# Projecting two head pairs at once in an attention and feed-forward kernel

## The chip, the cores and the metric

The kernel runs on one core of a Trainium2 chip. The metric is the device time of one execution in microseconds (us); lower is better. A core has five engines that run side by side and meet at semaphores: TensorE (PE; its weight loads are listed apart, as PEld), VectorE (DVE), ScalarE (ACT), GpSimd (POOL) and SyncE (SP), which here only starts DMA transfers. Sums of products land in PSUM, which has eight banks of 512 float32 values in each of 128 partitions.

## The reference, cut to what matters

Four batches of 1024 rows with 128 columns are normalised; the result goes through causal attention with 16 heads of width 64 and, beside it, through a quantised layer with ternary weights. Everything is float32.

```python
x = L0_attn_query                       # (4, 1024, 128)
xn = _layernorm(x)
# attention, B=4, S=1024, H=16, DH=64
q, k, v = split_heads(xn @ Wq), split_heads(xn @ Wk), split_heads(xn @ Wv)
w = softmax(einsum('bhqd,bhkd->bhqk', q, k) / DH + causal)
w = w * clip((arange(s) + span_val * s) / (RAMP + 1), 0, 1)
w = w / (sum(w, -1) + 1e-8)
attn = merge_heads(einsum('bhqk,bhkd->bhqd', w, v)) @ Wo      # Wo (1024, 128)
# feed-forward
x_int = clip(round(xn / scale), -127, 127)
ffn = nan_to_num(x_int * scale) @ (ternary_weight - 1).T + bias
return x + attn + ffn
```

The product with `Wo` is a sum over heads. A pair of heads gives 128 of its 1024 inputs, and the kernel adds what each pair brings to the rows of `x`.

## The kernel before, in words

The work is cut into 32 head pairs (8 for each batch), and one round of the program handles a pair. Each engine has a written order of units for a round (`PE_PLAN`, `ACT_PLAN`, `DVE_PLAN`, `POOL_PLAN`, lines 36 to 41), other orders for the start (`PE_FIRST` and so on) and for the last round (`PE_LAST`, `POOL_LAST`). A plus behind a unit means the next pair, a minus the pair before; `walk` writes the orders out.

The units, with their lines: Q and K project the queries and keys (881 to 885); M0 to M11 are the products from which the row maxima come (912), which DVE's R0 to R11 read (732, 736); V makes the values (899 to 901) and DVE's Vs weighs them (718); S0 to S11 are the scores of one block of keys (939), which ACT's E0 to E11 turn into `prob` (541); POOL's L cuts the diagonal blocks (448) and its A sums `prob` for the denominators (471, 475); G3, G7 and G11 are the products of `prob` with the values (956); D0 and D1 the denominators of the two halves of the queries (968); DVE's o divides (768) into `o_sb`; Y0 and Y1 are the output projection of a half (995), and DVE's Ya0 and Ya1 add it to `x_sb` (777). In the last pair of a batch the feed-forward products (983) go into the same bank ahead of Y.

Six PSUM banks form `ring`, three slots of two banks. The units Q, K, M, V and S take the slots in the order of the program, so each waits until the unit three places before it has been read (`slot_left`): behind S by its exponential, behind M by its maxima. In the middle of a round that order is S5 S6 M5 M6 M7 S7 M8, later S8 S9 S10 M9 M10 M11 S11. The bank `beside` carries T, D, X, W, F and Y one after the other (`beside_left`); `pv` takes the products of `prob` with the values. Y reads `o_sb`, one buffer for each half.

Units of a round on PE, around the change: `S5 S6 M5+ Y1- M6+ M7+ S7 D0 G3 M8+ S8 S9 S10 M9+ Y0 M10+ M11+ S11 G7`. A Y is four float32 products, each of which runs as two instructions.

At the start PE computes the maxima of pair 0 with idle products between them, I0 to I8 (1001): products of constants whose result is not used, two instructions each. `xn_sb` holds all four normalised batches, and parts of it first hold the raw weights `w_raw` and `wv_raw`, from which POOL makes the low parts `w2` (398) and `wv2` (431).

Of the kernel before, what the change touches and what calls it, by code (L numbers as in the profile page):

```python
# [32 lines left out]

PE_PLAN = ("T Q+ K+ X0 X1 W G11- M0+ M1+ S0 S1 S2 M2+ D1- M3+ V+ S3 S4 M4+ S5 S6 M5+ Y1- M6+ M7+ S7 D0 G3 "
           "M8+ S8 S9 S10 M9+ Y0 M10+ M11+ S11 G7")
ACT_PLAN = "Z Qhi+ Khi+ X0 X1 E0 E1 E2 ln1- ex1- E3 E4 E5 E6 E7 ln0 ex0 E8 E9 E10 E11"
# [1 line left out]
            "R9+ R10+ Ya0 R11+ Rc+")  # L40
POOL_PLAN = "L0 A0 L1 A1 L2 A2 L3 A3 A4 A5 A6 A7 L8 L9 L10 L11 A8 A9 A10 A11 B"

PE_FIRST = ("Q+ K+ M0+ M1+ M2+ I0+ M3+ I1+ M4+ I2+ M5+ I3+ M6+ I4+ M7+ I5+ M8+ I6+ M9+ I7+ M10+ I8+ M11+ Q++ T+ "
            "K++ S0+ S1+ S2+ V+")
DVE_FIRST = ("Qlo+ Klo+ R0+ R1+ R2+ R3+ R4+ R5+ R6+ R7+ R8+ R9+ R10+ R11+ Rc+ Tc+ Qlo++ Klo++ keys+ Vs+")
ACT_FIRST = "xf0+ Qhi+ xf1+ Khi+ rest+ keys+ wv+ Qhi++ Khi++ E0+ E1+ E2+"
# [13 lines left out]


STEP_OF = {1: "stats1", 2: "var1+", 3: "norm1a", 4: "norm1b", 5: "stats2", 6: "stats3", 7: "var2",
           8: "rstd2", 9: "norm2a", 10: "norm2b", 11: "norm3a", 12: "norm3b"}


def happens(name, i):

    if name in ("X0", "X1"):
        return i % PAIRS_OF_BATCH == 4 + int(name[1:]) and i < N_PAIRS - PAIRS_OF_BATCH
    if name == "W":  # L70
        return i == 1
    if name == "F1":
        return i == LAST
    if name[0] == "I":
        return i == 0
    if name == "q":
        return i % PAIRS_OF_BATCH < PAIRS_OF_BATCH - 1
    if name == "Z":
        return i in STEP_OF
    if name == "B":  # L80
        return i in (6, 11, 14)
    if name == "store":
        return i % PAIRS_OF_BATCH == PAIRS_OF_BATCH - 1
    return True
# [43 lines left out]
def attention_ffn(nc, x_dram, wq_dram, wk_dram, wv_dram, wo_dram, span_dram, tern_dram, bias_dram,  # L128
# [11 lines left out]
    with ctx:  # L140
# [4 lines left out]
            return ctx.enter_context(nc.semaphore(name))  # L145

        x_sb = sb("x_sb", [P, NB, D])
        xn_sb = sb("xn_sb", [P, NB * P])
        x1 = [sb(f"x1_{n}", [P, S], F32R) for n in range(2)]
        x2 = [sb(f"x2_{n}", [P, S], F32R) for n in range(2)]  # L150
        xf = sb("xf", [P, S])
        fq = sb("fq", [P, S])

        w_raw = [xn_sb[:, (B - 2 + n) * S:(B - 1 + n) * S] for n in range(2)]
        wv_raw = xn_sb[:, S:2 * S]
# [17 lines left out]
        v_sb = [sb(f"v_{p}", [P, KB, 4, DH]) for p in range(2)]  # L173
        NPROB = 8
        prob = [sb(f"prob_{n}", [P, 2, HALF]) for n in range(NPROB)]
        psumd = [sb(f"psumd_{c}", [P, 2, HALF]) for c in range(2)]

        minus_one, plus_one = psumd[0][0:1, :, :], psumd[1][0:3, :, :]
        lnden = sb("lnden", [P, HALF])
        r0 = sb("r0", [P, HALF])  # L180
        rden = sb("rden", [P, HALF])
        o_sb = [sb(f"o_{c}", [P, HALF]) for c in range(2)]
        rowmax = [sb(f"rowmax{p}", [P, P]) for p in range(2)]
        rowmax2 = [sb(f"rowmax2_{p}", [P, 2, HB]) for p in range(2)]
        maxrow = sb("maxrow", [2 * KB, P], F32R)
# [119 lines left out]
        def _(sp):  # L305
# [52 lines left out]
            for name, i in walk(SP_PLAN, SP_FIRST):  # L358
                if name == "mrow":
                    place_maxrow(i, i % 2)  # L360
                elif name == "kext":
                    place_key_weights(i, i % 2)
                else:
                    b = i // NPB
                    sp.wait_ge(y_added, halves_upto(i, 0))
                    store(b, 0, HB)
                    sp.wait_ge(y_added, halves_upto(i, 1))
                    store(b, HB, KB)
            sp.wait_ge(out_stored, 16 * 2 * B)

# [1 line left out]
        def _(pool):  # L372
# [105 lines left out]
            for name, i in walk(POOL_PLAN, "", POOL_LAST):  # L478
                if name[0] == "L":
                    select(i, int(name[1:]))  # L480
                elif name[0] == "A":
                    add(i, int(name[1:]))
                else:
                    add_bias((6, 11, 14).index(i) + 1)

        @block.scalar
        def _(act):
# [109 lines left out]
        def _(dve):  # L597
# [29 lines left out]

            def normalise(b, n0, n1):
                for n in range(b * KB + n0, b * KB + n1):
                    v.tensor_scalar(xn_sb[:, n * P:(n + 1) * P], x_sb[:, n, :], mv[:, n, 0:1],  # L630
                                    rstd[:, n:n + 1], ALU.subtract, ALU.mult).then_inc(xn_done, 1)

            def turned(b, c, src):
# [19 lines left out]

            def quantise(b, step):

                over = xn_sb[:, b * S:(b + 1) * S].bitcast(U32)
                if b or step > 1:
                    dve.wait_ge(fq_step, b * FQ_STEPS + (step - 1))
                else:
                    dve.wait_ge(lnw_split, 2)  # L660
                if step == 1:
                    dve.wait_ge(xf_done, 2 * b + 2)
                    ins = v.tensor_scalar(fq[:, :], xf[:, :], sc[:, 5:6], ACT_QB, ALU.mult, ALU.min)
                elif step == 2:
# [12 lines left out]

            def layer_norm_rest(step):

                if step[:5] == "stats":  # L680
                    statistics(int(step[5:]))
                elif step == "var1+":
                    variances(KB, 2 * KB)
                    rstd_finish(2, slice(KB, 2 * KB))
                elif step == "var2":
                    variances(2 * KB, NB)
                elif step == "rstd2":
                    rstd_finish(3, slice(2 * KB, NB))
                else:
                    if step == "norm1a":  # L690
                        dve.wait_ge(w_lo_done, 4)
                        dve.wait_ge(wv_lo_done, 1)
                    n0 = HB * "ab".index(step[5])
                    normalise(int(step[4]), n0, n0 + HB)

            def key_weights():

# [66 lines left out]
            def normalise_values(i, c):  # L764

                dve.wait_ge(rden_done, halves_upto(i, c))
                dve.wait_ge(pv_done, tiles_upto(i, HB - 1 if c == 0 else NT - 1))
                v.scalar_tensor_tensor(out=o_sb[c][:, :], in0=pv[:, :], scalar=-1.0, in1=rden[:, :],  # L768
                                       op0=ALU.mult, op1=ALU.mult).then_inc(o_done, 1)

            def add_output(i, c):

                b = i // NPB
                dve.wait_ge(y_ready, halves_upto(i, c))
# [49 lines left out]
        def _(pe):  # L824
# [19 lines left out]
            def beside_left(name, i):  # L844
# [7 lines left out]
                elif unit[0] == "D":  # L852
                    pe.wait_ge(rden_done, halves_upto(j, int(unit[1:])))
                elif unit[0] == "Y":
                    pe.wait_ge(y_added, halves_upto(j, int(unit[1:])))
# [208 lines left out]
```

## Time and profile before

| | |
|---|---|
| Median of 3 runs | 1015.55 us (1015.36 to 1018.13) |
| Profiled execution | 1013.19 us |
| Its span, first to last instruction | 1011.5 us |
| PE busy | 987.6 us, 98% |
| DVE busy | 766.3 us, 76% |
| POOL busy | 708.9 us, 70% |
| ACT busy | 455.0 us, 45% |
| Granted TensorE clock, mean | 1.000 |

The span begins with the first instruction and ends with the last one. Busy shares are means over the whole span. PE's instructions are pipelined, so one starts before the one ahead has ended: what PE spends on a unit is read from the start of its first instruction to the start of the next unit's.

### The profile page before, as it was taken

What the parts mean: (1) busy time and instruction counts of PE and PEld (TensorE: products, weight loads), DVE (VectorE), ACT (ScalarE), POOL (GpSimd) and SP (SyncE); (2) the same over time, 40 slices, a digit from 0 to 9 for tenths busy, and PEclk for the clock granted to TensorE, in tenths of its full rate; (3) what the DMA queues carried; (4) which work ended last, traced back from release to release, by engine and by line L of the source; (5) the groups of instructions that cost most, each with busy time, mean ns of one, the idle gap of its engine ahead of it and who ended that gap; (6) DMA issues with size and microseconds to landing.
All of it is one profiled execution on the core that took longest, in us unless ns stands there. A gap on an engine that the chain in (4) does not pass through costs nothing.

```text
span 1011.5 us, 19162 instructions
## 1 busy us (share of the span) xinstructions
PE 987.6 (98%) x7087; PEld 626.0 (62%) x7087; DVE 766.3 (76%) x1734; ACT 455.0 (45%) x607; POOL 708.9 (70%) x650
## 2 busy tenths in 40 slices
PE   7899999999999999999999999999999999999998
PEld 3565665666665666666666666666666666665654
DVE  8778788878788888877767877777877777777752
ACT  4344454444454444454444454444454444454442
POOL 8576767678766668767767677667766667767673
PEclk9999999999999999999999999999999999999999
DMA  6000000000000000000000000000000000000000
GB/s 174 3 3 2 2 2 2 2 2 3 2 22 2 3 2 3 1 3 2 3 12 12 2 3 2 2 3 2 2 2 24 2 3 2 1 2 2 2 1 22
DMA packets 16117, 8.52 MB, mean 8 GB/s; under 512 B 5388, under 2 KB 15628, under 8 KB 16024
## 3 DMA queue, kind: packets, MB, share of 16 engines
q1 hardware_dynamic: 15416, 7.16, 2.7%
q8 instruction: 57, 0.93, 0.4%
q14 instruction: 36, 0.29, 0.1%
q10 hardware_dynamic: 608, 0.14, 0.1%
HBM read 4.33 MB, written 2.10 MB: 6 GB/s over the span
## 4 chain that ended last, share of the span: by engine, by line
PE 84%; DVE 11%; issue 3%; DMA 1%; ACT 1%; SPq 0%; DVEq 0%; ACTq 0%
PE pv L956 25%; PE ring L939 24%; PE ring L912 12%; PE beside L995 7%; PE beside L968 6%; DVE v L718 3%; PE ring L885 3%; PE ring L881 3%; PE ring L882 3%; DVE ring L732 2%; DVE beside L756 2%; PE pv L1001 1%; PE beside L983 1%; PE beside L919 1%; DVE rowmax L732 1%
## 5 line engine op out<-in xcount | busy, mean ns | idle before, releaser
L541 ACT ACTIVATE prob<-ring 128x1024 f32<-128x1024 f32 (+3 forms) x384 | 294.3, 812 | 352.1 <-PE ring L939 337.1
L475 POOL TENSOR_TENSOR psumd<-psumd,prob 128x512 f32<-128x512 f32 (+1 forms) x252 | 410.5, 1629 | 28.3 <-POOL psumd L475 0.4
L732 DVE CUSTOM_DVE_ANT_0 ring<-ring,causal 128x128 f32<-128x128 f32 (+3 forms) x512 | 240.4, 516 | 98.0 <-PE ring L912 97.4
L939 PE MATMUL ring<-q,k 64*128 64x512 f32 (+3 forms) x2304 | 279.1, 348 | 3.6 <-DMA mrow<-maxrow 2.4
L956 PE MATMUL pv<-prob,v 128*64 128x512 f32 (+3 forms) x1536 | 267.2, 490 | 0.0
L448 POOL TENSOR_SCALAR_AFFINE_SELECT prob<-prob 128x256 f32<-128x256 f32 x256 | 107.0, 419 | 207.4 <-ACT prob L541 205.2
L939 PEld LDWEIGHTS ring<-q,k 64*128 64x128 f32 x2304 | 192.5, 185 | 39.1 <-DVE rowmax L732 5.2
L956 PEld LDWEIGHTS pv<-prob,v 128*64 128x64 f32 x1536 | 104.7, 137 | 153.6 <-issue 141.9
L471 POOL TENSOR_TENSOR psumd<-prob 128x768 f32<-128x768 f32 x64 | 135.2, 2112 | 43.3 <-ACT prob L541 38.6
L736 DVE TENSOR_REDUCE rowmax<-ring 128x2 f32<-128x1024 f32 x128 | 153.7, 1222 | 13.6 <-PE ring L912 10.3
L912 PE MATMUL ring<-k,q 64*128 64x512 f32 (+3 forms) x768 | 143.2, 409 | 8.7 <-DVE v L718 6.2
L939 PE MATMUL ring<-mrow,kext 64*128 64x512 f32 (+3 forms) x768 | 132.6, 341 | 0.0
L912 PEld LDWEIGHTS ring<-k,q 64*128 64x128 f32 x768 | 64.7, 184 | 81.3 <-ACT prob L541 27.6
L530 ACT ACTIVATE q<-ring 128x1024 fp32r<-128x1024 f32 x32 | 32.9, 1028 | 150.9 <-PE ring L885 150.9
L939 PEld LDWEIGHTS ring<-mrow,kext 64*128 64x128 f32 x768 | 72.8, 185 | 8.3
L995 PE MATMUL beside<-wo,o 128*128 128x128 f32 x512 | 72.6, 285 | 4.0 <-DVE o L768 2.7
L756 DVE TENSOR_TENSOR beside<-beside,r 128x512 f32<-128x512 f32 x63 | 45.0, 715 | 38.9 <-ACT r L552 38.9
L995 PEld LDWEIGHTS beside<-wo,o 128*128 128x128 f32 x512 | 62.0, 191 | 18.8 <-issue 12.0
L732 DVE DVE_READ_ACCUMULATOR2_ANT rowmax<- 128x1 f32 x512 | 72.3, 141 | 0.0
L707 DVE TENSOR_TENSOR q<-ring,q 128x1024 fp32r<-128x1024 f32 x32 | 39.1, 1222 | 43.0 <-ACT q L530 43.0
L968 PE MATMUL beside<-psumd,ones 128*64 128x512 f32 x252 | 68.0, 618 | 0.0
L881 PE MATMUL ring<-x,w 128*128 128x512 f32 x128 | 52.9, 414 | 0.0
(112 smaller groups left out, 945.6 us busy)
## 6 DMA issues: line engine op xcount, KB each, us to landing
x_sb<-in_L_attn_query SPq DMA_DIRECT2D x4, 512.0 KB, 5.4
kext<-kext SPq DMA_DIRECT2D x128, 4.0 KB, 1.7
out<-x_sb SPq DMA_DIRECT2D x8, 256.0 KB, 2.3
mrow<-maxrow SPq DMA_DIRECT2D x64, 4.0 KB
xn_sb<-in_L_attn_Wv SPq DMA_DIRECT2D x1, 512.0 KB, 5.6
wo<-in_L_attn_Wo SPq DMA_DIRECT2D x1, 512.0 KB, 7.2
xn_sb<-in_L_attn_Wq SPq DMA_DIRECT2D x1, 448.0 KB, 3.4
xn_sb<-in_L_attn_Wk SPq DMA_DIRECT2D x1, 448.0 KB, 4.1
```

The lines of the kernel that those rows point to most:

```text
L448: g.affine_select(out=d, in_=d, compare_op=ALU.is_ge, fill=0.0, base=0, pattern=[[0, 2], [1, P]], channel_multiplier=-1).then_inc(sel_done, 1)
L471: g.tensor_tensor(acc[:, :, lo:HALF], before[:, :, lo:HALF], pr[:, :, lo:HALF], ALU.add).then_inc(acc_done, 2)
L475: g.tensor_tensor(acc[:, :, lo:HALF], acc[:, :, lo:HALF], pr[:, :, lo:HALF], ALU.add).then_inc(acc_done, 1)
L541: a.activation(prob[n % NPROB][:, :, lo:HALF], ring[:, slot(f"S{t}", i), :, lo:HALF], ACT.Exp, scale=1.0 / DH).then_inc(exp_done, 1)
L732: last = v.tensor_tensor_reduce(out=ring[:, s, h, 0:n], in0=ring[:, s, h, 0:n], in1=causal[:, HALF - n:HALF], scale=1.0, scalar=MASKED, op ...
L736: last = v.tensor_reduce(dst[:, :, 0], ring[:, s, :, 0:n], axis=AX, op=ALU.max)
L881: t_.matmul(ring[:, s, c, :], w1[n][:, cols], xa[:, rows], start=True, stop=False)
L912: last = t_.matmul(ring[:, s, h, 0:n], q1[p][rows, j * P:(j + 1) * P], k1[p][rows, k0:k0 + n], start=True, stop=True)
L939: last = t_.matmul(ring[:, s, h, lo:HALF], k[p][rows, keys], q[p][rows, cols], start=(at == 0), stop=(at == len(parts) - 1))
L956: last = t_.matmul(pv[h * DH:(h + 1) * DH, lo:HALF], v_sb[i // 2 % 2][:, kb, i % 2 * 2 + h, :], prob[(i * NT + t) % NPROB][:, h, lo:HALF], ...
L968: last = t_.matmul(out[h * DH:(h + 1) * DH, :], ones[:, :], psumd[c][:, h, :], start=True, stop=not direct)
L995: last = t_.matmul(beside[:, k * P:(k + 1) * P], o_sb[c][:, k * P:(k + 1) * P], wo[:, i % NPB, :], start=not with_ffn, stop=(not with_ffn ...
```

## The change

Y of a pair is no longer issued for every pair. In the rounds where the odd pair's Y0 and Y1 fall due, one group takes both pairs: for each of the four row blocks the product of the even pair and that of the odd pair are added up in the same place of `beside`, sixteen instructions for eight. An odd round therefore has no Y1 and a Y0 of two pairs, an even round has a Y1 of two pairs and no Y0. The rest of the round's order on every engine stays. DVE adds half as many results to `x_sb`, and `o_sb` gets a second set of buffers.

`xn_sb` becomes two buffers of one batch each, and the normalisation of batch 3 moves from rounds 11 and 12 to 16 and 17 (its bias from 14 to 18). The raw weights go into the first three `prob` buffers, so E0 of pair 0 now waits until POOL has read them. The idle products between the maxima have half the columns, and I6 to I8 are left out.

```diff
-PE_FIRST = ("Q+ K+ M0+ M1+ M2+ I0+ M3+ I1+ M4+ I2+ M5+ I3+ M6+ I4+ M7+ I5+ M8+ I6+ M9+ I7+ M10+ I8+ M11+ Q++ T+ "
+PE_FIRST = ("Q+ K+ M0+ M1+ M2+ I0+ M3+ I1+ M4+ I2+ M5+ I3+ M6+ I4+ M7+ I5+ M8+ M9+ M10+ M11+ Q++ T+ "
...
-           8: "rstd2", 9: "norm2a", 10: "norm2b", 11: "norm3a", 12: "norm3b"}
+           8: "rstd2", 9: "norm2a", 10: "norm2b", 16: "norm3a", 17: "norm3b"}
...
+    if name[0] == "Y":
+        return i % 2 == 1
...
-        xn_sb = sb("xn_sb", [P, NB * P])
+        xn_sb = [sb(f"xn{n}", [P, S]) for n in range(2)]
...
+        w_raw = [prob[n][:, :, :].rearrange("p c n -> p (c n)") for n in range(2)]
+        wv_raw = prob[2][:, :, :].rearrange("p c n -> p (c n)")
...
-        o_sb = [sb(f"o_{c}", [P, HALF]) for c in range(2)]
+        o_sb = [[sb(f"o_{p}_{c}", [P, HALF]) for c in range(2)] for p in range(2)]
...
+        def outputs_upto(i, c):
+            return halves_upto(i // 2, c)
...
+                if n == 0:
+                    act.wait_ge(w_lo_done, 4)
+                    act.wait_ge(wv_lo_done, 1)
...
-                    if step == "norm1a":
-                        dve.wait_ge(w_lo_done, 4)
-                        dve.wait_ge(wv_lo_done, 1)
+                    b = int(step[4])
+                    if b > 1:
+                        dve.wait_ge(turned_ready, 2 * (b - 2) + 2)
...
+                if i >= 2:
+                    dve.wait_ge(y_ready, outputs_upto(i - 2, c))
-                v.scalar_tensor_tensor(out=o_sb[c][:, :], in0=pv[:, :], scalar=-1.0, in1=rden[:, :],
+                v.scalar_tensor_tensor(out=o_sb[i % 2][c][:, :], in0=pv[:, :], scalar=-1.0, in1=rden[:, :],
...
                 for k in range(HB):
-                    last = t_.matmul(beside[:, k * P:(k + 1) * P], o_sb[c][:, k * P:(k + 1) * P],
-                                     wo[:, i % NPB, :], start=not with_ffn, stop=(not with_ffn or k == HB - 1))
+                    for j in (i - 1, i):
+                        last = t_.matmul(beside[:, k * P:(k + 1) * P], o_sb[j % 2][c][:, k * P:(k + 1) * P],
+                                         wo[:, j % NPB, :], start=(k == 0 and j < i and not with_ffn),
+                                         stop=(k == HB - 1 and j == i))
...
-            def idle_products():
+            def idle_products(n):
 
-                t_.matmul(pv[:, :], ident[:, :], causal[:, :], start=True, stop=True)
+                t_.matmul(pv[:, 0:n], ident[:, :], causal[:, 0:n], start=True, stop=True)
...
                 elif name[0] == "I":
-                    idle_products()
+                    idle_products(2 * P)
```

Elsewhere waits that counted Y for every pair count it by `outputs_upto`, and readers of `xn_sb` take the buffer of their batch.

## Rows read from the trace of the kernel before

**Rows 1.** The page's first part: busy us, share of the span, instructions.

```profile
PE 987.6 (98%) x7087; PEld 626.0 (62%) x7087; DVE 766.3 (76%) x1734; ACT 455.0 (45%) x607; POOL 708.9 (70%) x650
```

**Rows 2.** Stretches: length, busy PE, PEld, DVE, ACT, POOL, granted clock, DMA share, GB/s.

```profile
17.00:34.00 17.00, 16.00 (x51) 6.32 (x52) 13.95 (x39) 6.58 (x7) 14.37 (x8) 1.00 0.37 90
34.00:39.00 5.00, 3.33 (x28) 2.73 (x28) 3.80 (x5) 2.19 (x3) 0.00 (x0) 1.00 0.04 8
853.85:883.79 29.94, 29.71 (x220) 18.92 (x218) 22.43 (x50) 13.70 (x18) 21.14 (x20) 1.00 0.01 1
```

**Rows 3.** Timeline, round 27 around Y1: M5, Y1, DVE's R5, M6, S7, D0.

```profile
869.12 0.39 PE L912 MATMUL ring<-k,q 64*128 64x512 f32 x2
869.57 1.13 PE L995 MATMUL beside<-wo,o 128*128 128x128 f32 x8
869.66 1.23 DVE L736 TENSOR_REDUCE rowmax<-ring 128x2 f32<-128x1024 f32 x1 [0.24 <-PE ring L912]
...
870.63 0.74 PE L912 MATMUL ring<-k,q 64*128 64x512 f32 x4
...
871.21 0.86 PE L939 MATMUL ring<-q,k 64*128 64x512 f32 x6
...
872.23 1.08 PE L968 MATMUL beside<-psumd,ones 128*64 128x512 f32 x4
```

**Rows 4.** Timeline, round 0: M5 and M6, M7, S7's weights, D0.

```profile
49.28 0.81 PE L912 MATMUL ring<-k,q 64*128 64x512 f32 x4
...
50.56 0.50 PE L912 MATMUL ring<-k,q 64*128 64x512 f32 x2 [0.47 <-ACT prob L541]
51.10 0.53 PEld L939 LDWEIGHTS ring<-q,k 64*128 64x128 f32 x6 [0.36 <-DVE rowmax L736]
...
52.23 1.08 PE L968 MATMUL beside<-psumd,ones 128*64 128x512 f32 x4
```

**Rows 5.** Timeline of PE, round 15, where F's eight instructions precede Y0: M9, M10.

```profile
514.08 0.38 PE L912 MATMUL ring<-k,q 64*128 64x256 f32 x2
...
516.37 0.67 PE L912 MATMUL ring<-k,q 64*128 64x384 f32 x4
```

**Rows 6.** Timeline, round 27 around Y0: E8 to E10, M9, Y0, R9's end, M10, S11.

```profile
876.73 2.21 ACT L541 ACTIVATE prob<-ring 128x1024 f32<-128x1024 f32 x3 [2.12 <-PE ring L939]
...
877.81 0.38 PE L912 MATMUL ring<-k,q 64*128 64x256 f32 x2
...
878.12 1.16 PE L995 MATMUL beside<-wo,o 128*128 128x128 f32 x8
...
879.12 0.14 DVE L732 DVE_READ_ACCUMULATOR2_ANT rowmax<- 128x1 f32 x1
879.21 0.67 PE L912 MATMUL ring<-k,q 64*128 64x384 f32 x4
879.72 0.45 PE L939 MATMUL ring<-q,k 64*128 64x128 f32 x6
```

**Rows 7.** Waits of DVE from 21.8 to 33.3 us: total, times, longest.

```profile
DVE ring L732 <- PE ring L912: 1.7, 3, 0.8
DVE rowmax L736 <- PE ring L912: 0.8, 3, 0.3
```

**Rows 8.** Timeline at the start: POOL makes `wv2`; ACT's E0 to E2.

```profile
27.09 2.35 POOL L431 TENSOR_TENSOR wv<-xn_sb,wv 128x1024 fp32r<-128x1024 f32 x1
...
38.18 2.22 ACT L541 ACTIVATE prob<-ring 128x1024 f32<-128x1024 f32 x3 [1.83 <-PE ring L939]
```

**Rows 9.** Timeline, round 31: Y1, POOL's A3, D0.

```profile
984.13 1.13 PE L995 MATMUL beside<-wo,o 128*128 128x128 f32 x8 [1.17 <-DVE o L768]
...
985.37 0.74 POOL L475 TENSOR_TENSOR psumd<-psumd,prob 128x256 f32<-128x256 f32 x1
...
987.26 1.08 PE L968 MATMUL beside<-psumd,ones 128*64 128x512 f32 x4
```

**Rows 10.** Groups by line and shape: DVE's Ya; busy us, mean ns.

```profile
L777 DVE TENSOR_TENSOR x_sb<-x_sb,beside 128x512 f32<-128x512 f32 x64 | 43.6, 681 | 7.5 <-PE beside L995 7.5
```

More of the change, by code:

```diff
@@ L80, in happens @@
     if name == "B":
-        return i in (6, 11, 14)
+        return i in (6, 11, 18)
     if name == "store":
@@ L152, in attention_ffn @@
         fq = sb("fq", [P, S])
-        w_raw = [xn_sb[:, (B - 2 + n) * S:(B - 1 + n) * S] for n in range(2)]
-        wv_raw = xn_sb[:, S:2 * S]
         w1 = [sb(f"w1_{n}", [P, H * DH], F32R) for n in range(2)]
@@ L364, in _ @@
                     b = i // NPB
-                    sp.wait_ge(y_added, halves_upto(i, 0))
+                    sp.wait_ge(y_added, outputs_upto(i, 0))
                     store(b, 0, HB)
-                    sp.wait_ge(y_added, halves_upto(i, 1))
+                    sp.wait_ge(y_added, outputs_upto(i, 1))
                     store(b, HB, KB)
@@ L483, in _ @@
                 else:
-                    add_bias((6, 11, 14).index(i) + 1)
+                    add_bias((6, 11, 18).index(i) + 1)
         @block.scalar
@@ L629, in normalise @@
                 for n in range(b * KB + n0, b * KB + n1):
-                    v.tensor_scalar(xn_sb[:, n * P:(n + 1) * P], x_sb[:, n, :], mv[:, n, 0:1],
+                    v.tensor_scalar(xn_sb[b % 2][:, (n - b * KB) * P:(n - b * KB + 1) * P], x_sb[:, n, :], mv[:, n, 0:1],
                                     rstd[:, n:n + 1], ALU.subtract, ALU.mult).then_inc(xn_done, 1)
@@ L654, in quantise @@
             def quantise(b, step):
-                over = xn_sb[:, b * S:(b + 1) * S].bitcast(U32)
+                over = xn_sb[b % 2][:, :].bitcast(U32)
                 if b or step > 1:
@@ L689, in layer_norm_rest @@
                 else:
-                    if step == "norm1a":
-                        dve.wait_ge(w_lo_done, 4)
-                        dve.wait_ge(wv_lo_done, 1)
+                    b = int(step[4])
+                    if b > 1:
+                        dve.wait_ge(turned_ready, 2 * (b - 2) + 2)
                     n0 = HB * "ab".index(step[5])
-                    normalise(int(step[4]), n0, n0 + HB)
+                    normalise(b, n0, n0 + HB)
             def key_weights():
@@ L773, in add_output @@
                 b = i // NPB
-                dve.wait_ge(y_ready, halves_upto(i, c))
+                dve.wait_ge(y_ready, outputs_upto(i, c))
                 dve.wait_ge(bias_added, b + 1)
@@ L854, in beside_left @@
                 elif unit[0] == "Y":
-                    pe.wait_ge(y_added, halves_upto(j, int(unit[1:])))
+                    pe.wait_ge(y_added, outputs_upto(j, int(unit[1:])))
                 elif unit[0] == "X":
@@ L864, in turn @@
                 for k in range(HB):
-                    n = b * KB + c * HB + k
-                    last = t_.transpose(out[:, k * P:(k + 1) * P], xn_sb[:, n * P:(n + 1) * P], ident[:, :])
+                    n = c * HB + k
+                    last = t_.transpose(out[:, k * P:(k + 1) * P], xn_sb[b % 2][:, n * P:(n + 1) * P], ident[:, :])
                 last.then_inc(turned_ready, 1)
@@ L988, in output_projection @@
                 with_ffn = i % NPB == NPB - 1
-                if i == 0 and c == 0:
+                if i == 1 and c == 0:
                     pe.wait_ge(wo_landed, 16)
@@ L994, in output_projection @@
                 for k in range(HB):
-                    last = t_.matmul(beside[:, k * P:(k + 1) * P], o_sb[c][:, k * P:(k + 1) * P],
-                                     wo[:, i % NPB, :], start=not with_ffn, stop=(not with_ffn or k == HB - 1))
+                    for j in (i - 1, i):
+                        last = t_.matmul(beside[:, k * P:(k + 1) * P], o_sb[j % 2][c][:, k * P:(k + 1) * P],
+                                         wo[:, j % NPB, :], start=(k == 0 and j < i and not with_ffn),
+                                         stop=(k == HB - 1 and j == i))
                 last.then_inc(y_ready, 1)
-            def idle_products():
-                t_.matmul(pv[:, :], ident[:, :], causal[:, :], start=True, stop=True)
+            def idle_products(n):
+                t_.matmul(pv[:, 0:n], ident[:, :], causal[:, 0:n], start=True, stop=True)
             pe.wait_ge(consts_done, NCONST)
             for n in range(NIDLE):
-                idle_products()
+                idle_products(HALF)
             for c in range(2):
@@ L1028, in _ @@
                 elif name[0] == "I":
-                    idle_products()
+                    idle_products(2 * P)
                 elif name[0] == "F":
```

## The prediction

> **What bounds the kernel now.** I read the page's first part, then the busy time by stretch, then the timeline round by round. Each round is weighed by the time from its first PE instruction to the next round's. PE is busy 98% of the span, DVE 76% [rows 1], and round 27, with nothing but its own work, takes 29.94 us, of which PE shows 29.71 as busy [rows 2]. So PE sets the pace, and the tempting reading is that whatever leaves PE shortens the round. That reading is the trap of this case. A busy PE may stand one ring slot away from a wait, and the order of the units, not the sum of them, decides what it may issue next. The Trainium skill says something near this: its page "Perfetto Trace Analysis", section "Identifying the Most-Contended Engine", holds matmul busy time a poor measure of headroom, because the instructions are pipelined. Round 27 agrees as far as it goes: busy weight loads are 18.92 us beside 29.71 of products [rows 2].
>
> Y stands twice in a round, and each time between units that wait for a ring slot. Ahead of Y1 stands M5, behind it M6, M7 and S7. M6 may start when E5 has emptied its slot, M7 when E6 has, S7 when R5 has read M5's maxima. In round 27 Y1 starts at 869.57 and M6 at 870.63, so Y1 takes 1.06 us [rows 3]. R5 starts at 869.66, after M5 alone, and ends at 870.89; S7 starts at 871.21 [rows 3]. Y1 thus fills nearly all the time that PE would wait for R5 anyway: the spare is 871.21 - 870.89 = 0.32 us. The same holds for Y0: it takes 878.12 to 879.21, 1.09 us, while ACT works through E8 to E10 until 876.73 + 2.21 = 878.94 and DVE's R9 ends at 879.12 + 0.14 = 879.26; S11, which takes the slot R9 empties, starts at 879.72 [rows 6]. The spare there is 0.46 us.
>
> **Products.** Their number does not change; only where they stand does. What eight more instructions in a group cost is seen where the feed-forward's eight run ahead of Y0: from M9 to M10 is 516.37 - 514.08 = 2.29 us in round 15 [rows 5] and 879.21 - 877.81 = 1.40 in round 27 [rows 6], so 0.89 us. I take 0.89 for each group of two pairs; nothing hides it, since everything behind it in the round merely gets later, and its slots empty earlier relative to PE.
>
> **Odd rounds: no Y1, a double Y0.** What the missing Y1 gives back has a direct witness. Round 0 has no pair before it, so it has no Y1 either. There PE goes from M5 to M6 at once, stands 0.47 us before M7 for ACT's exponential, and S7's weights wait for DVE's maxima until 51.10 [rows 4]. From M5 to D0 it takes 52.23 - 49.28 = 2.95 us [rows 4] against 872.23 - 869.12 = 3.11 with a Y1 [rows 3]: 0.16 given back of 1.06. Part of the spare of 0.32 is lost at the semaphore (some 0.05), and S7 behind a wait takes longer: 52.23 - 51.10 = 1.13 us to D0, against 1.02 in round 27, as its weights weren't loaded ahead. Bounds: 0.16 from below, 0.27 if that restart cost nothing. I take 0.16, which is measured. An odd round costs 0.89 - 0.16 = +0.73 us.
>
> **Even rounds: a double Y1, no Y0.** No round of before lacks Y0, so its return is bounded by the rows: nothing from below; from above, S11 at R9's end 879.26 + 0.05 = 879.31 instead of 879.72, that is 0.41. With the restart of 0.10 that S7 shows it is 0.31, and I take that, because S11 too would then stand behind a DVE wait. M10 and M11 wait for E9 and E10, which are done by 878.94 [rows 6], ahead of R9. An even round costs 0.89 - 0.31 = +0.58.
>
> Rounds 1 to 30 are fifteen of each: 15 x (0.73 + 0.58) = +19.65 us. Round 0 only loses its Y0: -0.31.
>
> **Round 31.** Its short order has no M units. Y1 of pair 30 goes; it had stood 1.17 us waiting for o and ran to the next unit, but D0 behind it also needs POOL's A3, which ends at 985.37 + 0.74 = 986.11, and D0 started at 987.26 [rows 9]. So 987.26 - 986.16 = 1.10 comes back. Its Y0 and its Y1 are both double, and the last one stands alone at the end: +1.78. Together +0.68.
>
> **The start.** While PE computes the maxima of pair 0, DVE waits for PE 1.7 + 0.8 = 2.5 us [rows 7], because an idle product stands ahead of each M. With half the columns and three fewer, M runs ahead and DVE's chain sets the time; the first T, the transfer of the maxima and S0 all hang on that chain. I take -2.5, with nothing and 2.5 as bounds. E0's new wait costs nothing: POOL ends `wv2` at 27.09 + 2.35 = 29.44, E0 started at 38.18 [rows 8], and 2.5 earlier it still has 6 us to spare.
>
> **The rest at nothing.** DVE does 32 fewer adds of 0.68 us [rows 10], some 22 us of its work, but PE waits for none of them: Ya1 stands behind R5 and Ya0 behind R10, and the chain M5, R5, S7 does not hold them. o's new wait is for a Y two pairs back, a round or more old. The normalisation of batch 3 moves with its small cost from two rounds to two others. The smaller `xn_sb` moves no work.
>
> **The sum.** 19.65 - 0.31 + 0.68 - 2.5 = +17.5 us. Against the profiled execution, 1013.19 us with a span of 1011.5, that is 1030.7. The median of the runs lies 2.36 above that execution, so I give the forecast on the median: 1015.55 + 17.5 = 1033 us. No change would be anything within 0.3%, 3 us.
>
> **Rivals.** First, the forecast's opposite: long groups pay. Every Y has an entry and an exit; two of them in a round take 2.15 us, and one double group 1.06 + 0.89 = 1.95 or 1.98. If PE were truly full, each pair of rounds would go from 4.30 to 3.93, and the sum would be -0.37 x 15 - 1.09 - 2.5 + 0.68 = -8.5, about 1007 us. It decides if the units behind an absent Y can start at once, which needs R5 and R9 to end some 0.7 us sooner. PE's 98% [rows 1] speaks for it, the waits of round 0 against it [rows 4]: chance 0.06. The Trainium skill, page "Perfetto Trace Analysis", section "Matmul Optimizations", wants products back to back in batches, which would favour this rival; no row here shows such a gain.
>
> Second, the absent groups give back just what the double ones add, through slack elsewhere: then only the ends are left, -2.5 - 0.3 + 0.7, about 1013.5 us. Same spot to look at, chance 0.05.
>
> Third, half is given back: 0.45 for each absent Y would make 15 x 0.88 = 13.2 less 2.1, near 1026.5. The 0.32 and 0.46 us of spare speak against it; chance 0.06.
>
> Fourth, the clock. From 17 to 34 us PE is busy 16.00 of 17.00 us with a granted clock of 1.00, its higher level of 2.4 GHz [rows 2], with nine idle products among the work. If PE fell to 1.2 GHz with fewer of them, S0 and what follows would take twice as long for a while, and the 2.5 us would be gone or worse: 1036 to 1038. Against it: from 34 to 39 us PE is busy only 3.33 of 5.00 us and the clock stays at 1.00 [rows 2]. Chance 0.08.
>
> **How the numbers follow.** The forecast has 0.75. Its own range is 1029 to 1038. From below both restart costs fall away: 15 x (0.62 + 0.48) = 16.5, less 0.41 for round 0 and 2.5, plus 0.68, is +14.3, or 1029.8, and the runs shown scatter by more than that last 0.8. From above an even round gets back nothing, +4.65, or 1037.7. The range to hold the time 8 times in 10 goes from the third rival to the fourth, 1026 to 1038; outside lie the first two, 0.11. Faster 0.06, same 0.05, slower 0.89.
>
> **What would show it.** In the profile after: odd rounds about 30.7 us and even ones about 30.5, where round 27 had 29.94; waits on PE before M7 (for E6) and S7 (for R5) in odd rounds, before M10, M11 or S11 in even ones; the double groups about 1.95 us long; S0 of pair 0 about 2.5 us sooner; DVE's L777 with 32 instructions. Rounds of 29.8 us without such waits would make the prediction wrong. Products that stand twice as far apart after 25 us would show the fourth rival.

## The result, and the profile after

The changed kernel takes 1034.85 us (median; 1032.96 to 1036.8) against 1015.45 (1014.73 to 1018.13) for the kernel before in the same rounds: 1.0186 times, with a 95% interval of 1.0156 to 1.0216. The forecast was 1033, the range 1026 to 1038. The execution that was profiled took 1032.96 us, with a span of 1031.2, 19.7 more than the span before.

The page's first part: PE works 6.0 us more than in [rows 1] and yet has fallen from 98% to 96% of the span.

```profile
PE 993.6 (96%) x7081; PEld 624.6 (61%) x7081; DVE 763.2 (74%) x1702; ACT 454.9 (44%) x607; POOL 708.6 (69%) x650
```

A round runs from its T (its first unit on PE, the transpose of the row maxima) to the next T. That splits the 19.7 us. "Expected" is what the prediction gave.

| stretch | before | after | difference | expected |
|---|---|---|---|---|
| up to S0 of pair 0 | 36.95 | 35.49 | -1.46 | -2.5 |
| S0 of pair 0 to T of round 1 | 26.86 | 26.83 | -0.03 | -0.31 |
| rounds 1 to 30 | 909.96 | 930.40 | +20.4 | +19.65 |
| round 31 | 37.69 | 38.50 | +0.81 | +0.68 |

The odd rounds give 11.34 us of the 20.4, 0.756 each; the even ones 9.11, 0.607 each. Rounds 27 and 28 have nothing but their own work; by stretch they answer to the last row of [rows 2] (columns as there). PE is busy 0.36 and 0.27 us more than there, and the rounds are 0.74 and 0.61 us longer (round 28 of before took 30.00 us itself; against that it is 0.55).

```profile
870.16:900.84 30.68, 30.07 (x220) 18.86 (x218) 21.85 (x49) 13.70 (x18) 21.16 (x20) 1.00 0.01 2
900.84:931.39 30.55, 29.98 (x220) 18.88 (x219) 23.47 (x49) 13.70 (x18) 21.50 (x20) 1.00 0.01 2
```

**Odd round, no Y1.** The timeline of round 27 from M5 to D0, to be held against [rows 3] and [rows 4] (M is L923 now, S is L950, D is L979):

```profile
885.43 0.88 PE L923 MATMUL ring<-k,q 64*128 64x512 f32 x4
...
886.72 0.50 PE L923 MATMUL ring<-k,q 64*128 64x512 f32 x2 [0.41 <-ACT prob L550]
887.25 0.53 PEld L950 LDWEIGHTS ring<-q,k 64*128 64x128 f32 x6 [0.35 <-DVE rowmax L745]
887.25 0.96 PE L950 MATMUL ring<-q,k 64*128 64x512 f32 x6
...
888.37 1.08 PE L979 MATMUL beside<-psumd,ones 128*64 128x512 f32 x4
```

M5 and M6 are one group now. M7 stands 0.41 us for ACT's E6, S7's weights wait for DVE's R5, and from M5 to D0 it takes 2.94 us, where it was 3.11 with a Y1 between. Round 0 of the kernel before had shown this figure (2.95) and the same two waits.

**The double groups.** The timeline of the same round around Y0, and of round 28 around Y1 (L1007):

```profile
893.96 0.39 PE L923 MATMUL ring<-k,q 64*128 64x256 f32 x2
894.28 2.05 PE L1007 MATMUL beside<-wo,o 128*128 128x128 f32 x16
896.26 0.67 PE L923 MATMUL ring<-k,q 64*128 64x384 f32 x4
...
916.57 2.02 PE L1007 MATMUL beside<-wo,o 128*128 128x128 f32 x16
918.52 0.74 PE L923 MATMUL ring<-k,q 64*128 64x512 f32 x4
```

To the next unit it is 1.98 us for Y0 and 1.95 for Y1; the single groups took 1.09 and 1.06.

**Even round, no Y0.** Round 28 from M9 on: M9, M10, S11, G7; POOL's A8, the last read of R11, Rc; and T of the next round. Rc is the last unit of DVE's order, line 743 before and 752 here: it combines the maxima of M8 to M11 with those of M4 to M7, and T transposes what it leaves.

```profile
925.71 0.38 PE L923 MATMUL ring<-k,q 64*128 64x256 f32 x2
926.40 0.99 PE L923 MATMUL ring<-k,q 64*128 64x384 f32 x4 [0.32 <-ACT prob L550]
927.23 0.53 PE L950 MATMUL ring<-q,k 64*128 64x128 f32 x6
927.80 3.65 PE L967 MATMUL pv<-prob,v 128*64 128x512 f32 x16
...
928.74 2.36 POOL L481 TENSOR_TENSOR psumd<-psumd,prob 128x1024 f32<-128x1024 f32 x1
929.34 0.14 DVE L741 DVE_READ_ACCUMULATOR2_ANT rowmax<- 128x1 f32 x1
929.51 1.61 DVE L752 TENSOR_TENSOR rowmax<-rowmax,rowmax 128x8 f32<-128x8 f32 x1
931.39 0.33 PE L930 MATMUL beside<-ident,rowmax 128*128 128x128 f32 x1
```

M10 stands 0.32 us for E9. From M9 to S11 it is 1.52 us instead of 1.91 [rows 6], so 0.39 of Y0's 1.09 comes back there; from S11, which follows the end of R9, to G7 it is then 0.57, where round 27 of before had 0.48 (G7 at 880.20). Together 0.30. The last two DVE rows matter below: Rc works on 8 numbers in each partition and takes 1.61 us.

**The start.** The timeline from the end of the maxima of pair 0: POOL's sum of `x_sb` and the bias, R11's last read, Rc, T, S0, and the weights of S2.

```profile
29.52 2.35 POOL L444 TENSOR_TENSOR x_sb<-x_sb,bias_b 128x1024 f32<-128x1024 f32 x1
...
30.02 0.14 DVE L741 DVE_READ_ACCUMULATOR2_ANT rowmax<- 128x1 f32 x1
30.19 1.71 DVE L752 TENSOR_TENSOR rowmax<-rowmax,rowmax 128x8 f32<-128x8 f32 x1
...
31.95 0.48 PE L930 MATMUL beside<-ident,rowmax 128*128 128x128 f32 x1 [1.37 <-DVE rowmax L752]
...
35.49 0.96 PE L950 MATMUL ring<-q,k 64*128 64x512 f32 x6 [0.51 <-DMA mrow<-maxrow]
...
37.36 0.42 PEld L950 LDWEIGHTS ring<-q,k 64*128 64x128 f32 x6 [0.29 <-DVE k L716]
```

The same place in the kernel before; POOL's sum there has ended (29.40 + 2.35 = 31.75) when Rc starts:

```profile
29.40 2.35 POOL L438 TENSOR_TENSOR x_sb<-x_sb,bias_b 128x1024 f32<-128x1024 f32 x1
...
33.16 0.14 DVE L732 DVE_READ_ACCUMULATOR2_ANT rowmax<- 128x1 f32 x1
33.33 0.17 DVE L743 TENSOR_TENSOR rowmax<-rowmax,rowmax 128x8 f32<-128x8 f32 x1
33.56 0.33 PE L919 MATMUL beside<-ident,rowmax 128*128 128x128 f32 x1 [0.27 <-DVE rowmax L743]
```

DVE's chain ended 3.14 us sooner. Rc took 1.71 us instead of 0.17 and gave 1.54 of it back; from T to S0 it is 3.54 us instead of 3.39.

TensorE's clock fell as well in this execution. By stretch (columns as in [rows 2]) the granted clock is 1.00 up to 26 us; then it falls to 1.2 GHz (0.50), by narrower stretches from about 28 to 35 us:

```profile
17.00:26.00 9.00, 7.50 (x32) 3.60 (x32) 8.82 (x22) 6.22 (x7) 8.70 (x6) 1.00 0.68 165
26.00:30.00 4.00, 3.06 (x10) 1.99 (x10) 4.00 (x16) 0.00 (x0) 3.92 (x3) 0.77 0.02 3
30.00:34.00 4.00, 2.63 (x8) 1.66 (x7) 3.27 (x5) 1.02 (x1) 1.87 (x1) 0.50 0.01 1
```

### The profile page after: what moved, and what is told of

Same layout as the page of the kernel before. It is cut to its first block, busy times and chain, and to the rows that moved or that the text cites. A ratio compares the mean times of both kernels' runs of the same rounds, so it can differ in the third digit from the quotient of the medians.

```text
span 1031.2 us, 19054 instructions
## 1 busy us (share of the span) xinstructions
PE 993.6 (96%) x7081; PEld 624.6 (61%) x7081; DVE 763.2 (74%) x1702; ACT 454.9 (44%) x607; POOL 708.6 (69%) x650
## 4 chain that ended last, share of the span: by engine, by line
PE 76%; DVE 10%; issue 5%; POOL 4%; ACT 4%; DMA 1%; SPq 0%; ACTq 0%; DVEq 0%; POOLq 0%
PE pv L967 24%; PE ring L950 20%; PE ring L923 9%; PE beside L1007 6%; PE beside L979 5%; ACT prob L550 3%; DVE v L727 3%; PE ring L896 3%; PE ring L892 3%; PE ring L893 3%; DVE ring L741 2%; POOL psumd L481 1%; DVE beside L765 1%; POOL psumd L477 1%; POOL prob L454 1%
## 5 line engine op out<-in xcount | busy, mean ns | idle before, releaser
L950 PE MATMUL ring<-q,k 64*128 64x512 f32 (+3 forms) x2304 | 282.1, 351 | 3.1 <-DMA mrow<-maxrow 1.2
L950 PEld LDWEIGHTS ring<-q,k 64*128 64x128 f32 x2304 | 190.3, 185 | 43.7 <-DVE rowmax L745 5.7
L923 PE MATMUL ring<-k,q 64*128 64x512 f32 (+3 forms) x768 | 151.1, 417 | 22.2 <-ACT prob L550 11.8
L950 PE MATMUL ring<-mrow,kext 64*128 64x512 f32 (+3 forms) x768 | 132.8, 341 | 0.0
L923 PEld LDWEIGHTS ring<-k,q 64*128 64x128 f32 x768 | 67.0, 183 | 104.8 <-ACT prob L550 59.1
L950 PEld LDWEIGHTS ring<-mrow,kext 64*128 64x128 f32 x768 | 72.9, 185 | 8.3
L979 PE MATMUL beside<-psumd,ones 128*64 128x512 f32 x252 | 68.0, 617 | 1.5 <-POOL psumd L481 1.5
L1007 PE MATMUL beside<-wo,o 128*128 128x128 f32 x512 | 64.6, 279 | 1.9 <-DVE o L779 1.4
L1007 PEld LDWEIGHTS beside<-wo,o 128*128 128x128 f32 x512 | 59.6, 192 | 8.5 <-issue 5.3
```

The source lines that it names most:

```text
L923: last = t_.matmul(ring[:, s, h, 0:n], q1[p][rows, j * P:(j + 1) * P], k1[p][rows, k0:k0 + n], start=True, stop=True)
L950: last = t_.matmul(ring[:, s, h, lo:HALF], k[p][rows, keys], q[p][rows, cols], start=(at == 0), stop=(at == len(parts) - 1))
L979: last = t_.matmul(out[h * DH:(h + 1) * DH, :], ones[:, :], psumd[c][:, h, :], start=True, stop=not direct)
L1007: last = t_.matmul(beside[:, k * P:(k + 1) * P], o_sb[j % 2][c][:, k * P:(k + 1) * P], wo[:, j % NPB, :], start=(k == 0 and j < i and not ...
```

## The experiments

The theory: the loss is in the ring's order. A Y had filled a wait for a slot; without it PE stands at the same slot for ACT or DVE. Its rivals: the loss comes from the start and its clock; or from the buffers and the moved normalisation; or the double groups cost more than single ones for a reason of their own. Four steps test this: parts of the change by themselves, other work put into the emptied places, the wait that this uncovered, and its controls. All ratios are to the kernel before, run beside it.

**Pairs without the shorter start.** The idle products as before, the rest as changed.

```diff
-PE_FIRST = ("Q+ K+ M0+ M1+ M2+ I0+ M3+ I1+ M4+ I2+ M5+ I3+ M6+ I4+ M7+ I5+ M8+ M9+ M10+ M11+ Q++ T+ "
+PE_FIRST = ("Q+ K+ M0+ M1+ M2+ I0+ M3+ I1+ M4+ I2+ M5+ I3+ M6+ I4+ M7+ I5+ M8+ I6+ M9+ I7+ M10+ I8+ M11+ Q++ T+ "
...
-                    idle_products(2 * P)
+                    idle_products(HALF)
```

> The change without its edit to the idle products: nine of them, full width, as before. Slot theory (the units behind an absent Y stand at ring slots, so little of it comes back): odd rounds 30.7 us and even ones 30.5, S0 of pair 0 at 36.95 as before, granted clock 1.00, about +20 us, 1035, with a scatter like that of the kernel before. Rival (the start, its idle products and the shared buffers make the loss): within 4 us of the kernel before, 1014 to 1019.

1038.90 us, ratio 1.0223 (1.0196 to 1.0251). Rounds 1 to 30 cost 20.3 us more than before, as in the changed kernel, and S0 to T(1) 26.58 us, 0.28 less than before. The loss is in the rounds, not in the start. That its profiled execution is slower than that of the changed kernel comes from its start: S0 at 40.00 us, not at 36.95 as expected. Its granted clock was low earlier, although its idle products were the full ones (the stretch, columns as above):

```profile
18.00:25.00 7.00, 6.79 (x11) 2.36 (x12) 4.36 (x18) 4.89 (x5) 6.70 (x6) 0.51 0.71 171
```

**The shorter start alone.** The kernel before with that one edit.

```diff
-PE_FIRST = ("Q+ K+ M0+ M1+ M2+ I0+ M3+ I1+ M4+ I2+ M5+ I3+ M6+ I4+ M7+ I5+ M8+ I6+ M9+ I7+ M10+ I8+ M11+ Q++ T+ "
+PE_FIRST = ("Q+ K+ M0+ M1+ M2+ I0+ M3+ I1+ M4+ I2+ M5+ I3+ M6+ I4+ M7+ I5+ M8+ M9+ M10+ M11+ Q++ T+ "
...
-                    idle_products()
+                    idle_products(2 * P)
```

> The kernel before with only the shorter idle products, I6 to I8 left out. Slot theory: rounds of 29.95 us as before. Were the clock to stay at its higher level, S0 of pair 0 would come 2.5 us sooner, 1013. If the clock falls as in the changed kernel, S0 comes about 1.5 us sooner in some runs and later than before in others, and the runs scatter over 3 to 4 us: 1013.5 to 1018. Rival (the start makes the loss): over 1025.

1013.75 us, ratio 0.9979 (0.9963 to 0.9995): 2.1 us gained by the ratio, 1.4 by the medians (1015.14 before), with clean rounds at 29.95 as before. So the start doesn't make the loss. The gain on the kernel before is small: the interval ends at 0.9995. In its profiled execution the clock was low from about 20 to 37 us and S0 came at 39.16, later than before.

**Shorter idle products, all nine kept.**

```diff
-PE_FIRST = ("Q+ K+ M0+ M1+ M2+ I0+ M3+ I1+ M4+ I2+ M5+ I3+ M6+ I4+ M7+ I5+ M8+ M9+ M10+ M11+ Q++ T+ "
+PE_FIRST = ("Q+ K+ M0+ M1+ M2+ I0+ M3+ I1+ M4+ I2+ M5+ I3+ M6+ I4+ M7+ I5+ M8+ I6+ M9+ I7+ M10+ I8+ M11+ Q++ T+ "
```

> The change with I6 to I8 put back, all idle products at half width. If fewer products before T let the clock fall: clock 1.00 throughout, S0 of pair 0 at 34.1 to 34.5, rounds as in the changed kernel (30.7 and 30.5), a scatter of 1 to 2 us, and 1031 to 1032.5. Rival (half width alone lets it fall): a granted clock below 1.00 between 25 and 40 us, S0 at 35.5 or later, 1033 to 1037 as in the changed kernel.

1038.92 us, ratio 1.0206 (1.0177 to 1.0236), S0 at 40.05 us. The three products don't hold the clock up. In its profiled execution it was low for 17 us, with PE shown busy throughout (columns as above):

```profile
20.00:37.00 17.00, 17.00 (x40) 8.37 (x41) 10.89 (x29) 3.94 (x5) 11.76 (x7) 0.51 0.18 43
```

Of its six executions four had a mean granted clock of 0.990 (1038.43 to 1040.14 us), one 0.997 (1034.07) and one 1.000 (1032.88): with the same products the clock falls in one execution and stays up in another.

**The buffers alone.** The changed kernel with a Y for every pair and the idle products as before.

```diff
...
-    if name[0] == "Y":
-        return i % 2 == 1
...
-            return halves_upto(i // 2, c)
+            return halves_upto(i, c)
...
-                    for j in (i - 1, i):
-                        last = t_.matmul(beside[:, k * P:(k + 1) * P], o_sb[j % 2][c][:, k * P:(k + 1) * P],
...
+                    last = t_.matmul(beside[:, k * P:(k + 1) * P], o_sb[i % 2][c][:, k * P:(k + 1) * P],
...
```

> The change with every pair projected by itself again and the idle products as before: what is left is the shared buffers of the normalised rows and the raw weights, the second set of o_sb, and the normalisation of batch 3 in rounds 16 and 17. Forecast: nothing, within 2 us of the kernel before, 1014 to 1018, rounds 16 and 17 up to 0.7 us longer and 11 shorter by as much. Rival (the sharing makes a wait): 3 us or more slower.

1016.79 us, ratio 1.0014 (1.0000 to 1.0029). Rounds 1 to 30 take 0.5 us more than before, round 11 being 0.65 shorter and rounds 16 and 17 0.29 and 0.32 longer. The buffers, the second `o_sb` and the moved normalisation cost next to nothing.

**The emptied places filled.** The changed kernel, but in odd rounds D0 stands between M5 and M6, and in even ones a quarter of G7 (G4) between M9 and M10, the rest (G5) at the end. No product is added or taken away.

```diff
-           "M8+ S8 S9 S10 M9+ Y0 M10+ M11+ S11 G7")
+           "M8+ S8 S9 S10 M9+ G4 M10+ M11+ S11 G5")
+PE_ODD = ("T Q+ K+ X0 X1 W G11- M0+ M1+ S0 S1 S2 M2+ D1- M3+ V+ S3 S4 M4+ S5 S6 M5+ D0 M6+ M7+ S7 G3 "
+          "M8+ S8 S9 S10 M9+ Y0 M10+ M11+ S11 G7")
...
+GROUP_OF = {"G3": range(0, 4), "G4": range(4, 5), "G5": range(5, 8), "G7": range(4, 8), "G11": range(8, 12)}
...
```

> The change with other work put where Y is absent: D0 between M5 and M6 in odd rounds, the first quarter of G7 between M9 and M10 in even ones; nothing is added or left out. Slot theory: the waits before M7, S7, M10, M11 and S11 are filled, odd and even rounds take 29.8 us, some 0.8 less each, 25 us in all, 1010. Rival (groups of sixteen products cost more than two of eight): rounds stay at 30.5 to 30.7, 1035.

1024.52 us, ratio 1.0085 (1.0062 to 1.0107): half of the loss is gone. The stretches of rounds 27 and 28:

```profile
863.01:892.93 29.92, 29.74 (x217) 18.58 (x217) 21.95 (x49) 13.59 (x18) 21.59 (x20) 1.00 0.01 2
892.93:923.59 30.66, 29.75 (x219) 18.79 (x218) 23.19 (x49) 13.69 (x18) 21.37 (x20) 1.00 0.01 2
```

The odd round is back at 29.92, as the theory had it. The even round is not: the wait for the slot is gone, yet the round takes 30.66. Its timeline shows another wait, at its end. M9, G4 and M10; POOL's A8; Rc; T of the next round:

```profile
917.80 0.38 PE L925 MATMUL ring<-k,q 64*128 64x256 f32 x2
918.12 1.08 PE L969 MATMUL pv<-prob,v 128*64 128x512 f32 x4
919.12 0.67 PE L925 MATMUL ring<-k,q 64*128 64x384 f32 x4
...
921.06 2.36 POOL L483 TENSOR_TENSOR psumd<-psumd,prob 128x1024 f32<-128x1024 f32 x1
922.23 1.21 DVE L754 TENSOR_TENSOR rowmax<-rowmax,rowmax 128x8 f32<-128x8 f32 x1
923.59 0.30 PE L932 MATMUL beside<-ident,rowmax 128*128 128x128 f32 x1 [0.67 <-DVE rowmax L754]
```

T waits 0.67 us for Rc, and Rc ends at 923.44, when POOL's A8 ends at 923.42. In round 28 of the changed kernel the two ends are 931.12 and 931.10, at its start 31.90 and 31.87. In round 27 of the kernel before, by its timeline, they are 883.53 and 883.51:

```profile
881.14 2.37 POOL L475 TENSOR_TENSOR psumd<-psumd,prob 128x1024 f32<-128x1024 f32 x1
...
882.88 0.65 DVE L743 TENSOR_TENSOR rowmax<-rowmax,rowmax 128x8 f32<-128x8 f32 x1
```

So a second theory for the even rounds: Rc doesn't end before the POOL sum that runs when it starts. Before, PE's G7 covered that; a quarter of G7 moved forward leaves less cover.

**T later.** The filled kernel, with T behind Q in nine odd rounds, the other place from which PE can take work while Rc is late.

```diff
...
+        if odd and i % 2 and i < LAST and i not in STEP_OF:
+            text = text.replace("T Q+", "Q+ T")
...
```

> As the filled version, with T behind Q in nine odd rounds (11, 13, 15, 19 to 29). In the filled version an even round ends with PE waiting at T for DVE's Rc, which ends with POOL's A8. If that wait is all that keeps the even rounds at 30.64 us: the nine even rounds ahead of a late T take about 29.9 from Q to Q, the odd ones stay at 29.9, and the time falls by 9 x 0.75 = 7 us, to 1017 or 1018. Rival (the quarter of G7 in the place of Y0 is no use, whatever T does): 1024.5 as in the filled version.

1018.54 us, ratio 1.0032 (1.0016 to 1.0047). From Q to Q round 28 now takes 29.81 us, and rounds 1 to 30 together 6.0 us less than in the filled kernel, for an expected 7. The wait for Rc is what held them.

**A8 earlier.** The filled kernel, with A8 ahead of L11 in even rounds, to end the sum before Rc.

```diff
+POOL_PLAN = "L0 A0 L1 A1 L2 A2 L3 A3 A4 A5 A6 A7 L8 L9 L10 A8 L11 A9 A10 A11 B"
+POOL_ODD = "L0 A0 L1 A1 L2 A2 L3 A3 A4 A5 A6 A7 L8 L9 L10 L11 A8 A9 A10 A11 B"
...
```

> As the filled version, with POOL's A8 ahead of L11 in even rounds, so that it is over before Rc is due. If Rc, a DVE instruction that reads two operands from SBUF, stands still while POOL's A8 runs: Rc takes under 0.3 us in even rounds where it took 1.21, even rounds fall from 30.64 to 29.9, 15 x 0.7 = 10 us, to 1014. Rival (Rc is slow by itself, or the slots keep the even rounds long): Rc stays at 1.2 us or even rounds at 30.6, 1024.5.

1032.18 us, ratio 1.0163 (1.0142 to 1.0184), even rounds 31.1: worse, against the expectation. The timeline of round 28, R11's last read, POOL's A9, Rc:

```profile
931.06 0.14 DVE L744 DVE_READ_ACCUMULATOR2_ANT rowmax<- 128x1 f32 x1
931.07 1.81 POOL L484 TENSOR_TENSOR psumd<-psumd,prob 128x768 f32<-128x768 f32 x1
931.24 1.67 DVE L755 TENSOR_TENSOR rowmax<-rowmax,rowmax 128x8 f32<-128x8 f32 x1
```

A8 did end sooner, but A9 began 0.17 us ahead of Rc, and Rc ended at 932.91 with A9 at 932.88. The edit missed its gap; it follows that Rc is tied to whichever sum is running, not to A8.

**No Rc.** The filled kernel, in which R8 to R11 start from the maxima of R4 to R7 (the scalar of their instruction), so that nothing is left to combine. T waits for R11.

```diff
...
-            "R9+ R10+ Ya0 R11+ Rc+")
+            "R9+ R10+ Ya0 R11+")
...
-                dst = maxes[:, :, j:j + 1] if k0 == 0 else rowmax2[p][:, :, j - HB:j - HB + 1]
+                dst = maxes[:, :, j:j + 1]
...
-                            scale=1.0, scalar=MASKED, op0=ALU.add, op1=ALU.max, accum_out=dst[:, h, :])
+                            scale=1.0, scalar=dst[:, h, :] if k0 else MASKED, op0=ALU.add, op1=ALU.max,
+                            accum_out=dst[:, h, :])
...
-                pe.wait_ge(rowmax_done, i + 1)
+                pe.wait_ge(max_read, (i + 1) * NM)
```

> As the filled version, without Rc: R8 to R11 start their maxima from those of R4 to R7, so that no DVE instruction with two operands in SBUF stands between R11 and T. If Rc, held until POOL's sum ends, is what keeps even rounds at 30.64 us: T comes when G5 is done, even rounds take 29.9, odd ones 29.9 as before, and the time is 1024.5 - 15 x 0.75 = 1013, level with the kernel before. Rival (the quarter of G7 does not fill the place of Y0): even rounds 30.6, 1024.

1013.80 us, ratio 0.9988 (0.9975 to 1.0002). Rounds 27 and 28 by stretch:

```profile
856.65:886.63 29.98, 29.71 (x220) 18.57 (x219) 21.57 (x48) 13.59 (x18) 22.21 (x21) 1.00 0.01 2
886.63:916.54 29.91, 29.69 (x219) 18.77 (x218) 22.18 (x48) 13.70 (x18) 20.79 (x19) 1.00 0.01 2
```

Rounds 1 to 30 are 1.3 us above the kernel before, of the 20.4 that the change had cost. (The changed kernel without Rc but with its places left empty was not run. There Rc was done 0.27 us before T in round 28, so Rc did not hold that round.) The interval reaches past 1, so this version is level with the kernel before, not shown to beat it.

**No Rc in the kernel before.** The same edit as a control.

```diff
-            "R9+ R10+ Ya0 R11+ Rc+")
+            "R9+ R10+ Ya0 R11+")
...
```

> The kernel before, without Rc in the same way: the control for the run beside it. In the kernel before T stands behind G7, which ends after Rc, so nothing waits for Rc: rounds of 29.95 us, the time that of the kernel before within 2 us. Rival (leaving out Rc shortens a round in any case): 0.3 us or more a round, below 1007.

1014.99 us, ratio 0.9986 (0.9973 to 0.9999); rounds 1 to 30 are within 0.1 us of before, so the 0.14% isn't in the rounds. Rc isn't waited for there, and what its removal gave to the filled kernel was the filled kernel's own wait.

**The moves alone.** The kernel before, every Y as it was, with D0 behind Y1 in odd rounds and G4 behind Y0 in even ones.

```diff
-           "M8+ S8 S9 S10 M9+ Y0 M10+ M11+ S11 G7")
+           "M8+ S8 S9 S10 M9+ Y0 G4 M10+ M11+ S11 G5")
+PE_ODD = ("T Q+ K+ X0 X1 W G11- M0+ M1+ S0 S1 S2 M2+ D1- M3+ V+ S3 S4 M4+ S5 S6 M5+ Y1- D0 M6+ M7+ S7 G3 "
+          "M8+ S8 S9 S10 M9+ Y0 M10+ M11+ S11 G7")
...
```

> The kernel before, unpaired, with D0 behind Y1 in odd rounds and the first quarter of G7 behind Y0 in even ones. Slot theory: there is no empty place to fill, so odd rounds stay at 29.95 us; in even rounds S11 and with it A8 and Rc come 0.8 later, T waits for Rc, about 30.6: 1015 + 15 x 0.7 = 1025. Rival (the moves shorten a round by themselves, and that is what the filled version gained): odd rounds near 29.2, below 1012.

1046.91 us, ratio 1.0303 (1.0283 to 1.0323). Even rounds take 30.84, somewhat more than was expected of G4 behind Y0. Odd rounds take 31.1, far from the expectation. The timeline shows why, Y1 and D0:

```profile
897.68 1.13 PE L997 MATMUL beside<-wo,o 128*128 128x128 f32 x8
899.64 1.08 PE L970 MATMUL beside<-psumd,ones 128*64 128x512 f32 x4 [0.83 <-DVE x_sb L779]
```

D0 and Y1 share the bank `beside`, and D0 stands 0.83 us until DVE's Ya1 has read it. As a control for the odd rounds this run says nothing. In the even rounds it says that moving the quarter of G7 gains nothing by itself.

## Why the prediction was right

**The odd rounds.** Expected +0.73, measured 0.756 on average, and 30.68 against 29.94 us in round 27. Both terms hold: the double group costs 1.98 where a single one cost 1.09 (0.89), and an absent Y1 gives back 0.17 of its 1.06 for an expected 0.16, with the waits for E6 and R5 that were named. The witness, round 0 of before, was worth more than the busy share. That the wait was the reason is shown by the filled kernel: D0 in that place brings the round to 29.92.

**The even rounds.** Expected +0.58, measured 0.607 on average; the absent Y0 gave back 0.30 for an expected 0.31. M10 stands for E9, and S11 follows where R9 has emptied its slot. The prediction named that wait and stopped there. Behind it stood a second one: Rc, held by POOL's sum, was done 0.27 us before T started in round 28, and the filled kernel ran into it at once. Without it, but with the emptied places filled, both kinds of round are back at 29.9 to 30.0.

**The sum of the rounds** came to 20.4 for 19.65. Rounds with nothing special gave 0.75 (odd) and 0.59 (even), which is half of the excess; most of the rest lies in round 23 alone, +1.14, and why is open. The moved normalisation shortens round 11 by about what it adds to 16 and 17.

**The start** is the term that was mis-sized: -1.46 for -2.5. The step "DVE's chain sets the time; the first T, the transfer of the maxima and S0 all hang on that chain" was right, and the chain gained even more, 3.14 us. What was missed is that Rc is part of it: 3.14 us sooner, it met POOL's sum of `x_sb` and the bias, which it had followed before, and 1.54 us went there. The last 0.15, from T to S0, goes with the lower clock: T itself took 0.48 us for 0.33. This is one execution against one in which the clock stayed at 1.00; over twelve executions the shorter start alone gave 2.1 us by its ratio.

**Round 0** gave -0.03 for -0.31. Where the clock was back up when K's low part was made, in the kernel with pairs alone, it gave -0.28. In the changed kernel S2's weights waited 0.29 us for that low part (DVE, line 716), which came late at the lower clock: K's products stood 0.43 us apart, 0.23 in the kernel before.

**Round 31** gave +0.81 for +0.68, and the rest at nothing holds to within 0.5 us (the rounds of the kernel with the buffers alone). DVE's adds halved as forecast, by the groups by line and shape, and nothing waited for what this freed:

```profile
L788 DVE TENSOR_TENSOR x_sb<-x_sb,beside 128x512 f32<-128x512 f32 x32 | 21.9, 685 | 19.3 <-PE beside L1007 19.3
```

**The rivals.** Long groups do cost less than two single ones, 1.95 or 1.98 against 2.15, 0.2 us for each pair; outside the group the order took back more. (The Trainium skill's page "Perfetto Trace Analysis", section "Matmul Optimizations", wants products back to back in batches because the engine scales its power with utilization. The granted clock was 1.00 in these rounds of both kernels, so the 0.2 us are no gain of that kind, and no run here shows one.) Even with both waits removed the gain of 0.37 for each pair of rounds doesn't show: 59.89 us for rounds 27 and 28 without Rc, 59.94 for the same two before. From start to start of PE's instructions in these two rounds, Y takes 3.93 us for 4.29 and the maxima 6.72 for 6.96, but the scores take 19.54 for 19.24, the products with the values 16.49 for 16.28 and the denominators 3.94 for 3.84. Why these became longer is open. That half would be given back, or all of it, fell with the rounds.

The fourth rival, the clock, came true in part. The clock fell, and the price that this rival named, 1036 to 1038 us, is what two of the four executions show: 1036.34 and 1036.80 at a mean granted clock of 0.990, beside 1032.96 and 1033.36 at 0.997 and 0.998. The profile is of the fastest, where the rows show 0.15 us of it before S0 and some 0.25 behind it. So the rounds are forecast by their mechanism, but that the median lies within 2 us of the forecast is partly luck: it is the middle between two kinds of execution, and four don't show how often each comes. The cause that the rival gave, fewer idle products, can be no more than a part of it: the clock falls without that edit too (last section).

## What to carry to other kernels

A busy engine with a fixed order may be full only because a unit happens to fill a wait; before taking one out, look for a round that lacks it already, and read what PE does there. When such a wait is removed, list what else ends just ahead of the next unit, on the other engines too (here Rc, 0.27 us ahead of T), because that sets the time next. If a unit must go, put another from the same round into its place, one that uses neither the slot nor the bank that is waited for.

## What the hardware showed

**A small DVE instruction that waits for POOL.** Rc took 0.17 us with POOL idle, 0.65 in round 27 of before, and 1.71 at the start of the changed kernel. Ten of the kept traces have an Rc, 320 in all. Seven found POOL idle and took 0.17 us each. The other 313 met a sum that had started 0.04 to 1.75 us earlier; they took 0.64 to 2.32 us, and every one ended 0.02 to 0.03 us after that sum. The Trainium skill's page "SBUF — State Buffer", section "Who interferes with whom", states that a DVE instruction with two SBUF inputs contends with a GpSimd instruction that reads SBUF, and that the one that issues first blocks the other until it is done. The rows agree: Rc reads two SBUF tensors, and in each of those cases the sum had started first. The chip's port itself was not measured here; that the wait goes when Rc goes is.

**The clock at the start.** In the profiled execution of the kernel before the granted clock was 1.00 throughout the start [rows 2]. It fell to 1.2 GHz (0.50) for a while within the first 51 us in the profiles of the changed kernel and of every other version but the moves alone, with full and with half idle products; S0 of pair 0 came at 35.49 to 41.34 us in these. There is one profile of each, but each timed execution is on record with its mean granted clock. The kernel before was run 63 times beside the experiments, and its clock was 0.990 to 1.000: at 1.000, five times, it took 1013.46 to 1014.40 us, at 0.990 1020.23 and 1020.91. So it falls in some executions of one and the same kernel, without any edit, and the profile of the kernel before is of one of the few in which it did not. The idle products have a share in it: with the shorter start as the only edit the median of these means was 0.991 in twelve executions, against 0.997 in the 17 of the kernel before run beside them. What sets it in one execution and not in the next is left open. It bears on some 3 us in the changed kernel and 7 in the kernel before, and not on the rounds: in every profile the clock was 1.00 from 51 us to the last 3 us of the span.
